# Audio tower block: the vector engine takes the second sequence's heads and the token probabilities, products and waits are put in another order

## The reference

```
q, k, v = token mix of x (16 tokens to 8, weights Wq, Wkv, biases bq, bkv)
h  = q*scale + softmax(q*scale . k^T) . v                    # per batch and position, over tokens
h  = h + attention(layernorm(h)): 12 query heads, 3 key heads of 64, rotary, softmax . V, then Wo
h  = h + gelu(layernorm(h) . in_weight^T + in_bias) . out_weight     # 192 -> 768 -> 192
```

## Time and profile before

| | us |
|---|---|
| median of 3 runs | 1063.11 (1062.52 to 1064.49) |
| the profiled execution | 1062.68 |
| its span | 1060.9 |
| PE busy | 981.5 (93%) |
| weight loads busy | 833.4 (79%) |
| DVE busy | 770.6 (73%) |
| ACT busy | 719.3 (68%) |
| POOL busy | 667.3 (63%) |

### The profile page before, as it was taken

The page is one execution under the profiler, slowest core; times in us unless marked ns, Lnnn a source line. Parts: engine busy times, 40 slices in busy tenths (PEclk is TensorE's granted clock), DMA queues, the critical chain, the costliest instruction groups (busy, mean ns, idle before and its releaser), DMA issues.

```text
span 1060.9 us, 25539 instructions
## 1 busy us (share of the span) xinstructions
PE 981.5 (93%) x7360; PEld 833.4 (79%) x7360; DVE 770.6 (73%) x1871; ACT 719.3 (68%) x2594; POOL 667.3 (63%) x967
## 2 busy tenths in 40 slices
PE   3668999999999999999999999999999999999986
PEld 2557788888888888888888888788788888888775
DVE  2577777787777778777777877777877777787761
ACT  2347677767767776776777677677677677767752
POOL 0556667666676766667676666767666667666660
PEclk7779999999999999999999999999999999999999
DMA  5034343444434344433334443434444343444341
GB/s 180 21 119 137 108 121 111 121 138 134 123 109 131 106 133 127 145 116 116 124 101 146 126 142 113 120 112 116 145 127 131 103 135 110 124 132 140 97 126 45
DMA packets 139935, 127.69 MB, mean 120 GB/s; under 512 B 30480, under 2 KB 123024, under 8 KB 139920
## 3 DMA queue, kind: packets, MB, share of 16 engines
q1 hardware_dynamic: 137632, 124.29, 39.5%
q10 hardware_dynamic: 2288, 3.21, 0.9%
HBM read 70.83 MB, written 56.62 MB: 120 GB/s over the span
## 4 chain that ended last, share of the span: by engine, by line
PE 40%; ACT 19%; DMA 16%; DVE 9%; issue 7%; SPq 6%; POOL 2%; ACTq 0%; DVEq 0%; POOLq 0%
PE ring L685 11%; ACT E L303 8%; DMA spill<-EB 8%; DMA ET<-spill 7%; PE ring L666 6%; SPq L244 6%; PE ring L744 4%; PE ring L853 3%; PE bank L701 3%; ACT G L384 3%; PE ring L784 3%; DVE EB L531 3%; ACT t_e L343 2%; PE ring L780 2%; PE bank L826 2%
## 5 line engine op out<-in xcount | busy, mean ns | idle before, releaser
L303 ACT ACTIVATE E<-ring,m_neg 128x128 f32<-128x128 f32 x768 | 272.4, 389 | 33.3 <-DVE m_neg L520 33.3
L423 POOL TENSOR_TENSOR E<-E,e_rcp 128x512 f32<-128x512 f32 x192 | 199.2, 1045 | 44.0 <-DVE e_rcp L540 42.7
L415 POOL TENSOR_TENSOR qkT<-rot_c,rot_s 128x256 f32<-128x256 f32 x256 | 187.7, 733 | 20.1
L303 ACT ACTIVATION_READ_ACCUMULATOR E<-ring,m_neg 128x1 f32 x768 | 175.1, 228 | 0.0
L701 PE MATMUL bank<-wout_sb,G 128*128 128x192 f32 x768 | 145.8, 327 | 2.8 <-ACT G L384 2.8
L413 POOL TENSOR_TENSOR rot_s<-rot_s,rope_qs 128x256 f32<-128x256 f32 x192 | 140.3, 730 | 9.1 <-DVE rot_s L508 7.3
L531 DVE STREAM_TRANSPOSE EB<-E 128x512 f32<-128x512 f32 x192 | 132.7, 694 | 17.2 <-POOL E L423 17.1
L853 PE MATMUL ring<-wo_sb,OT 128*128 128x192 f32 x768 | 135.5, 326 | 0.1
L520 DVE TENSOR_REDUCE m_neg<-ring 128x4 f32<-128x512 f32 x192 | 126.7, 675 | 9.8 <-PE ring L720 9.8
L701 PEld LDWEIGHTS bank<-wout_sb,G 128*128 128x128 f32 x768 | 123.5, 190 | 4.1 <-ACT G L384 3.3
L853 PEld LDWEIGHTS ring<-wo_sb,OT 128*128 128x128 f32 x768 | 124.9, 190 | 0.8 <-issue 0.7
(11 more groups left out here) (133 smaller groups left out, 2546.1 us busy)
## 6 DMA issues: line engine op xcount, KB each, us to landing
spill<-EB SPq DMA_DIRECT2D x64, 512.0 KB, 2.7
ET<-spill SPq DMA_DIRECT2D x256, 128.0 KB, 2.8
spill<-EB SPq DMA_DIRECT2D x64, 256.0 KB, 2.0
ET<-spill SPq DMA_DIRECT2D x256, 64.0 KB, 2.3
x_sb<-in_x_dram SPq DMA_DIRECT2D x64, 192.0 KB, 2.5
out_dram<-out_sb SPq DMA_DIRECT2D x64, 96.0 KB, 2.3
x_sb<-in_x_dram SPq DMA_DIRECT2D x64, 64.0 KB, 2.3
w_raw<-in_w_att_dram ACTq DMA_DIRECT2D x2, 608.0 KB, 5.8
```

The source lines that it names most:

```text
L303: last = nc.scalar.activation(E[:, a, s * P:(s + 1) * P], RING[a][:, s * P:(s + 1) * P], ACT.Exp, bias=m_neg[:, a, s:s + 1], accum_out=e_s ...
L415: nc.gpsimd.tensor_tensor(qkT[:, b, :, a], rot_c[:, b, :, a], rot_s[:, b, :, a], ALU.add).then_inc(q_out, 1)
L423: nc.gpsimd.tensor_tensor(e, e, r, ALU.mult).then_inc(prob_out, 1)
```

## The change

1. The copies of sequence 1's heads out of PSUM go from ACT to DVE, between the second and the third maximum, with a semaphore of their own (`OT1_out`).
2. The scaling of the token probabilities goes from ACT (two instructions) to DVE (one, 128 x 256, multiplied by a broadcast of the inverted sums).
3. ACT takes the exponentials of two groups of heads, not one, ahead of the copy of the turned token probabilities.
4. POOL multiplies the third group of probabilities ahead of the feed-forward layer norm's root, and copies `h2` ahead of the token layer norm's root.
5. DVE takes the layer norm statistics of sequence 1 after the first block transposition and the third inverted sum, applies that norm after all three transpositions, and adds `h_next` ahead of the maxima of sequence 1.
6. PE's `ffn_second` is split otherwise: parts 2 and 3 of sequence 0 stay where 2 to 5 were, and parts 4 and 5 with 0 to 2 of sequence 1, and then 3 to 5, follow where before 0 to 3 and then 4 and 5 were.
7. The hidden products of a bank use HH for both halves first, and then HL.
8. GELU begins with the third bank, and the waits of `tok_qk` and `v_projected` on it ask for two and four of the six instead of six and two; `tok_scores` no longer waits for `vq_out`.

```diff
+GELU_ORDER = (4, 5, 0, 1, 2, 3)
...
@@ scalar
-                    act.wait_ge(t_rcp, n + 1)
-                    for a in range(2):
-                        nc.scalar.activation(t_a[:, a, :], t_e[:, a, :], ACT.Copy,
-                                             scale=t_rs[:, a:a + 1]).then_inc(t_norm, 1)
-                if ffn:
-                    heads_out(1, p - 1)
                 if att:
                     score_exp(0, 0)
+                    score_exp(0, 1)
                 if tok:
                     act.wait_ge(aT_mm, n + 1)
                     nc.scalar.copy(t_aT[:].rearrange("p a c -> p (a c)"), TOK_AT).then_inc(aT_out, 1)
                 if att:
-                    score_exp(0, 1)
                     score_exp(0, 2)
...
-                    heads_out(0, p)
+                    heads_out(p)
...
-                    for m in range(NM):
+                    for m in GELU_ORDER:
...
@@ gpsimd
                     probs(0, 1, p)
+                    probs(0, 2, p)
                 if ffn:
                     rstd2(2 * p, 1)
-                if att:
-                    probs(0, 2, p)
+                    wait_apart(pool, pool_passed, (h2_out, 2 * p), (res_out, p - 1))
+                    nc.gpsimd.tensor_copy(h2_kept[:], h2[:]).then_inc(h2_copied, 1)
...
@@ vector
+                def heads_out(q):
+                    for b, c in enumerate((slice(0, 512), slice(512, DQ))):
+                        heads = (c.stop - c.start) // P
+                        dve.wait_ge(pv_mm, 4 * q + 2 + b + 1)
+                        nc.vector.tensor_copy(OT[:, 1, c].rearrange("p (h i c) -> p h i c", h=heads, i=NB),
+                                              RING[1][:, c].rearrange("p (i h c) -> p h i c", h=heads, i=NB)
+                                              ).then_inc(OT1_out, 1)
...
                     nc.vector.reciprocal(t_rs[:], t_sum[:]).then_inc(t_rcp, 1)
+                    dve.wait_ge(t_rcp, n + 1)
+                    need(dve, aT_mm, n)
+                    nc.vector.tensor_tensor(t_a[:], t_e[:], t_rs[:].rearrange("p (a o) -> p a o", o=1).broadcast_to([P, 2, P]),
+                                            ALU.mult).then_inc(t_norm, 1)
...
@@ tensor
-                        pe.wait_ge(gelu_out, 6 * (p - 2) + 2)
+                        pe.wait_ge(gelu_out, 6 * (p - 2) + 4)
...
-                        pe.wait_ge(gelu_out, 6 * (p - 1))
+                        pe.wait_ge(gelu_out, 6 * (p - 2) + 2)
...
-                    pe.wait_ge(vq_out, 4 * n + 4)
...
+                        for m in (2 * j, 2 * j + 1):
+                            for w, h in ((FH1, h1h), (FL1, h1h), (F2S, h2h)):
+                                nc.tensor.matmul(bank[:, (m % 2) * DP:(m % 2 + 1) * DP], w[:, m * P:(m + 1) * P], h,
+                                                 start=(m % 2 == 0 and w is FH1), stop=False)
+                        if j == 0:
+                            pe.wait_ge(HL_out, p)
...
-                            pe.wait_ge(OT_out, 4 * q + 2 * a + t // 4 + 1)
+                            pe.wait_ge(OT_out if a == 0 else OT1_out, 2 * q + t // 4 + 1)
...
                 if fin:
-                    ffn_second(0, p - 2, range(2, NM))
+                    ffn_second(0, p - 2, range(2, 4))
                 if ffn:
                     output(1, p - 1)
                 if tok:
                     tok_h()
                 if fin:
-                    ffn_second(1, p - 2, range(4))
+                    ffn_second(0, p - 2, range(4, NM))
+                    ffn_second(1, p - 2, range(3))
                 if att:
                     scores(1)
                 if ffn:
                     hn_turned()
                 if fin:
-                    ffn_second(1, p - 2, range(4, NM))
+                    ffn_second(1, p - 2, range(3, NM))
```

More of the change, by code:

```diff
@@ L605, in step @@
                     sums_inverted(0, 2, p)
+                if ffn:
+                    attention_stats(1, 2 * p)
+                if att:
                     blocks_turned(0, 1, p)
+                if att:
+                    blocks_turned(0, 2, p)
                 if ffn:
@@ L610, in step @@
                     normalise(h2, mv2, rs2, hn, 1).then_inc(hn_out[1], 1)
+                if tok:
+                    dve.wait_ge(h_mm, n + 1)
+                    need(dve, h_moved, n)
+                    nc.vector.tensor_tensor(h_next[:], TOK_H.rearrange("p (a d) -> p a d", a=2), t_q[:],
+                                            ALU.add).then_inc(h_out, 1)
                 if att:
-                    blocks_turned(0, 2, p)
                     key_max(1, (0,))
```

39 lines of the change are left out of this document (16 added, 23 removed).

## The result

The changed kernel takes 1029.93 us (median of 4 runs, 1028.92 to 1030.54) where the kernel before takes 1062.82 (4 runs, 1060.48 to 1064.49) on the same chip: ratio 0.9691, 95% interval 0.9671 to 0.9711, 32.9 us less. The forecast was 1042.6 with a range of 1026 to 1057. The direction and the range held.

What follows compares the result with a forecast made beforehand. ACT's late start was taken as the last wait before the spill that PE's transfers need. An earlier spill (0.61) plus 0.05 gave 0.66 a step; over 30.5 steps 20.1 us, so 1042.6 us, range 1026 to 1057.

Steps and rivals of the forecast that it cites:

- first rival: More comes free: without POOL's turn-taking with DVE a step gains 0.96 us, giving 1033 us; chance 0.19.
- The wait that ended last: ACT's late exponentials, behind scalings and copies, held up the spill; starting them 1.8 us earlier lets it go 0.61 earlier.
- PE's wait for `hn`: PE waiting for the applied feed-forward norm: 0.6 us expected; more, with transfers no longer waited for, would refute the forecast.
- POOL's start: POOL's first group of probabilities, begun at 521.10 before, was to begin at 521.3 and hold back the first transposition.
- Turn-taking: DVE's scaling of token probabilities and POOL's rotation, both reading SBUF, wait for each other: 0.3 us taken for each.
- `vq_out` wait: PE's `tok_scores` waiting for `vq_out`: 4.3 us over 27 steps, 0.16 a step, expected to go.
- second spill: It follows the first sooner, so the eight transfers behind need not wait for it: 0.05 us more a step.
- The waits of PE: PE's waits for the last GELU and `vq_out` both go: 0.3 us in all, 0.1 of it reaching POOL's rotation.
- GELU wait: PE's `tok_qk` waiting for the last GELU: 0.26 us a step, gone once only two GELUs are asked for.
- The costs on DVE: DVE's two head copies take 0.68 and 0.42 us, some 1.0 together; `hn` takes 0.38 instead of 0.93.
- `t_a`: DVE's scaling of the token probabilities, one 128 x 256 instruction, from 517.65 to 518.35 with turn-taking.
- third rival: Slower: the spill waits for DVE's head copies through PE's `output`, deciding from a 1.64 us first copy; 1075 us, chance 0.07.

Runs made afterwards that it cites:

- e4: The changed kernel with sequence 1's heads copied by ACT again, ahead of the exponentials: 1052.03 us, 22.9 us slower than the changed kernel.
- e9: The changed kernel with the GELU order and the two waits on GELU as before: 1034.83 us, 5.8 us slower than the changed kernel.
- e2: The changed kernel with the wait of `tok_scores` for `vq_out` put back: 1033.89 us, 4.5 us slower than the changed kernel.
- e1: The kernel before with only the wait of `tok_scores` for `vq_out` removed: 1055.11 us, 7.3 us faster than the kernel before.
- e6: The changed kernel with DVE scaling the token probabilities a second time into an unread buffer: 1048.64 us, 20.6 us slower than the changed kernel.
- e7: The changed kernel with `ffn_second` split as before, four parts of sequence 0 ahead of `output`: 1036.90 us, 9.0 us slower than the changed kernel.
- e10: The changed kernel with sequence 1's statistics on DVE moved behind the second block transposition: 1036.49 us, 8.0 us slower than the changed kernel.
- e5: The changed kernel with the token probabilities scaled by ACT again, in two instructions: 1030.37 us, ratio 0.9700 to the kernel before.

## Why the prediction was right, and where its size was off

The mechanism was right, and the size was short in two places: 0.33 a step, some 9 us, and the start, some 6 us. That the time still lies in the range is in part luck. Its lower end was set for the first rival, which knows nothing of the start; without the start's share the time would be about 1036.

**The wait that ended last: right.** The sum held that the spill comes earlier by what is taken from ACT, that DVE then waits at the residual for PE's `output`, about 1.0 us, and that PE keeps up. Measured: 1.15 at the residual, and PE still waits for the transfers. PE's wait for `hn` is 0.26, less than the 0.6 I had allowed for. In the frame of the rows before, with 505.12 as the step's first projection, `output`'s end was foreseen at 521.65 and came at 502.68 - 486.21 + 505.12 = 521.59. e4 shows that the heads' copy is the main part.

**The mis-sized term is POOL's start.** I had the first transposition wait for POOL's first group, ending 522.34, and begin at 522.37. It does wait for it. But in the same frame POOL begins at 501.97 - 486.21 + 505.12 = 520.88, 0.22 earlier than before and 0.42 earlier than I said, and the transposition, 0.15 behind that group's end, at 522.07: 0.30 of the gain. Two estimates made this up. Turn-taking cost POOL 0.18 (0.91 against 0.73) where I took 0.3, and POOL's start as a whole moved by 0.40 where I took 0.1. e9 shows where from: with the waits on GELU back, POOL's first group starts 0.35 later (16.11 against 15.76), and e2 adds 0.07 for the `vq_out` wait. From the first to the second transposition it is 1.27 and not 1.38, 0.11 more; to the spill 0.83 and not 0.79. 0.61 + 0.30 + 0.11 - 0.04 = 0.98. The 0.05 for the second spill is not seen. Over 27 steps the difference of 0.33 is 8.9 us. My first rival had named this size (0.96 a step without turn-taking), but by a way that the runs don't show, since turn-taking was there.

**The missed term is the start.** I priced the `vq_out` wait by the loop (4.3 us in 27), and did not look at its one occurrence outside of that window. It was 6.15 us long, and e1 and e2 show that the start's 6.5 us come with it. In the changed kernel's loop the wait itself costs nothing that can be seen (e2).

**The waits of PE: right in length, wrong in what they are worth.** I had the GELU wait at 0.26 and let 0.1 of PE's waits reach POOL, and so the sum. e9 gives 0.25 a step for it: everything behind it, down to the spill, hangs on PE. This is the same term as POOL's start, seen from its cause.

**The end: missed.** The GELU order lets PE stand 1.5 us longer once. The rest is the lower clock there, which no part of the prediction had; why it fell in one kernel and not in the other stays open.

**The costs on DVE: right but for `t_a`.** The copies take 0.68 and 0.41 (1.00 together) and `hn` 0.38 where it was 0.93. `t_a` takes 0.50, where I had 0.7 with the turn-taking.

**The third rival** needed a first copy of 1.64 us to decide. e6 shows its mechanism at work. DVE's queue ahead of the first copy was made 0.9 longer, and PE stood for 0.79 of that, since PE reaches `output` just as the copy is ready. `output` starts 0.87 later and the first transposition 0.70, so the slack against POOL is 0.17 (e7 has 0.19), where I had 0.3.

What stays open: the exponentials' new order on ACT, POOL's third group ahead of the root, and the order of HH and HL in the hidden products were not undone one by one. Of the last the trace shows that PE's gap ahead of the first HL product is gone: it follows its neighbour by 0.12 (508.93 after 508.81), where it was 0.31. The single undoings (e4, e7, e9, e2) add up to 23 + 9 + 6 + 5 = 43 us, more than the whole 33: the parts need one another.

## What to carry to other kernels

When work is moved off the engine that ends last, ask at once what is late next and whether the same edit moves that too. The heads' copy alone brought 2 us, because PE's `output` and the statistics stood right behind; within the whole change, where these have moved too, it is worth 23. Look up a wait that is to be removed at every place where it occurs, the first one above all: 0.16 us in the loop was 6.15 at the start. And where several engines arrive within 0.2 us of one another, a further step in the same direction costs: e10 made the spill's way shorter and was 8 us slower, since `hn` and `xn` came later for it.

## What the runs showed of the hardware

DVE and POOL, both reading from SBUF, took turns, and the price depends on where the instructions meet. DVE's 128 x 256 product of two SBUF tensors took 0.50 in the changed kernel and POOL's instruction beside it 0.91, 0.18 longer than the 0.73 of the earlier trace rows and of e5. Done twice (e6), the second took 0.94, since it stood until POOL's instruction had ended at 507.87. An instruction with a single tensor as input did the same. DVE's timeline in the changed kernel,

```profile
511.98 1.09 DVE L484 TENSOR_SCALAR xn<-h_next,mv,rs 128x192 f32<-128x192 f32 x1 [0.61 <-POOL rs L439]
...
513.21 0.37 DVE L484 TENSOR_SCALAR xn<-h_next,mv,rs 128x192 f32<-128x192 f32 x1
```

and POOL's:

```profile
511.91 1.04 POOL L418 TENSOR_TENSOR E<-E,e_rcp 128x512 f32<-128x512 f32 x1
```

The one that began 0.07 after POOL's took 1.09 and ended 0.12 after it; its twin, with POOL idle, took 0.37. The Trainium skill (SBUF — State Buffer, section "SBUF: two separate sides") calls the pair of ports that they share an exclusive lock, held for the whole instruction, for a DVE instruction with two SBUF inputs or in a two-port mode. The durations of DVE agree: each time it waits for what is left of POOL's. POOL lost only 0.18, though 0.32 of DVE's 0.50 were left when it began. Which mode the single-input instruction ran in, no run here shows. So 0.3 for each, as I took it, was too high for POOL here and far too low for DVE in e6. In the changed kernel `xn` loses 0.7 us a step this way, and PE does not wait for it; in e10 it does (0.95 for turning `xn`, 0.66 in the changed kernel). Moving the two apart was not tried.
